# A transformer block on one core: three copies of residuals on GpSimd taken out, with x, x1 and x2 in two buffers each

## The reference, cut to what matters

```
x = x + xattn(ctx, layernorm(x), mask, ...)     # 16 heads of 16, 256 keys from ctx, bias by distance
x = x + attn(layernorm(x), ...)                 # normalizes once more, 16 heads of 64, unit-length q and k,
                                                # two null keys, linear bias, causal
x = x + ffn(layernorm(x), ...)                  # 8 experts of rank 16 on one shared hidden layer of 1024, top 2
return x                                        # (64, 64, 256), float32
```

## Time and profile before

| | |
|---|---|
| Median of 3 runs | 1583.59 us |
| The profiled execution, its own time | 1582.87 us |
| Its span, first to last instruction | 1581.1 us |
| TensorE busy | 1406.5 us, 89% |
| VectorE busy | 1243.2 us, 79% |
| ScalarE busy | 1123.3 us, 71% |
| GpSimd busy | 491.3 us, 31% |
| Mean granted clock of TensorE | 0.968 of full |
| DMA engines, mean rate | 70 GB/s |

### The profile page before, as it was taken

How to read it: one execution, slowest core, us unless ns; L and a number is a source line. 1 busy time by engine, 2 the same in 40 slices (tenths; PEclk the granted TensorE clock), 3 DMA queues, 4 the chain that set the end, 5 groups by cost and what they waited for, 6 DMA issues and landing times.

```text
span 1581.1 us, 42702 instructions
## 1 busy us (share of the span) xinstructions
PE 1406.5 (89%) x16891; PEld 1024.8 (65%) x16891; DVE 1243.2 (79%) x3414; ACT 1123.3 (71%) x3091; POOL 491.3 (31%) x589
## 2 busy tenths in 40 slices
PE   3378999999999999999999999999999999999975
PEld 1245776766677666666776766667666666776744
DVE  2647888888888888888888888888888888888862
ACT  2656778777777787777778777777787777778741
POOL 2122233333323332333233333323332333233220
PEclk7589999999999999999999999999999999999987
DMA  8522212222221122222212222221122222212100
GB/s 199 171 68 75 64 42 63 70 78 79 79 79 47 43 69 78 79 78 79 70 39 60 69 78 79 78 79 53 42 65 78 78 78 79 75 37 57 52 4 7
DMA packets 80918, 110.49 MB, mean 70 GB/s; under 512 B 7592, under 2 KB 62928, under 8 KB 80720
## 3 DMA queue, kind: packets, MB, share of 16 engines
q1 hardware_dynamic: 80720, 107.76, 23.8%
HBM read 69.66 MB, written 29.69 MB: 63 GB/s over the span
## 4 chain that ended last, share of the span: by engine, by line
PE 58%; ACT 29%; DVE 8%; issue 3%; DMA 1%; POOL 1%; SPq 0%; POOLq 0%; ACTq 0%; DVEq 0%
ACT S L924 7%; PE ps_a L507 7%; PE ps_a L508 6%; PE ps_a L509 6%; ACT av L986 5%; ACT pT L936 4%; PE ps_f L507 4%; PE ps_f L509 4%; PE ps_f L508 4%; PE ps_t L597 3%; PE ps_a L728 3%; PE ps_o L609 3%; ACT aqT L1040 3%; ACT a_work L997 2%; PE ps_s L507 2%
## 5 line engine op out<-in xcount | busy, mean ns | idle before, releaser
L924 ACT ACTIVATE S<-S,x_nmx 128x256 f32<-128x256 f32 x512 | 257.0, 506 | 29.9 <-DVE x_nmx L1204 28.3
L1204 DVE CUSTOM_DVE_ANT_0 S<-ps_s,bias 128x256 f32<-128x256 f32 x512 | 201.8, 418 | 65.2 <-PE ps_s L587 63.7
L597 PE MATMUL ps_t<-ident,S 128*128 128x128 f32 x1024 | 188.9, 287 | 42.8 <-ACT S L924 26.3
L1568 POOL TENSOR_TENSOR a_len<-a_len,half 128x16 f32<-128x16 f32 x64 | 212.4, 3318 | 5.3
L936 ACT ACTIVATE pT<-ps_t 128x256 f32<-128x256 f32 x512 | 174.2, 380 | 40.6 <-PE ps_t L597 35.8
L597 PEld LDWEIGHTS ps_t<-ident,S 128*128 128x128 f32 x1024 | 115.3, 143 | 86.3 <-ACT S L924 69.5
L1573 POOL TENSOR_TENSOR aN<-aS,a_sum 128x128 f32<-128x128 f32 x32 | 30.0, 936 | 368.7 <-DVE a_sum L1305 368.7
L587 PE MATMUL ps_s<-kst,qst 128*128 128x256 f16 x512 | 115.5, 279 | 17.8 <-DMA qst<-q_hbm 15.4
L507 PE MATMUL ps_f<-zT,f_loraB 128*128 128x128 f16 x512 | 102.8, 220 | 8.7 <-ACT f_h L1028 8.6
L508 PE MATMUL ps_f<-zT,f_loraB 128*128 128x128 f16 x512 | 102.4, 219 | 0.0
L509 PE MATMUL ps_f<-zT,f_loraB 128*128 128x128 f16 x512 | 102.4, 219 | 0.0
(11 more groups left out here) (244 smaller groups left out, 4643.6 us busy)
## 6 DMA issues: line engine op xcount, KB each, us to landing
ctxT<-in_ctxT SPq DMA_DIRECT2D x32, 512.0 KB, 4.8
k_hbm<-kT SPq DMA_DIRECT2D x32, 512.0 KB, 3.0
kst<-k_hbm SPq DMA_DIRECT2D x32, 512.0 KB, 4.4
kst<-negm SPq DMA_DIRECT2D x32, 256.0 KB, 3.1
q_hbm<-qT SPq DMA_DIRECT2D x64, 128.0 KB, 1.8
kst<-k_hbm SPq DMA_DIRECT2D x32, 256.0 KB, 3.4
qst<-q_hbm SPq DMA_DIRECT2D x32, 256.0 KB, 4.6
x_ld<-in_x SPq DMA_DIRECT2D x32, 128.0 KB, 4.2
```

The lines of the kernel that those rows point to most:

```text
L597: last = turn(ps_t[t % 2][:, c * P:(c + 1) * P], S[:, t % S_BUFS, c * P:(c + 1) * P], ident[:])
L924: go(S[:, t % S_BUFS, :], S[:, t % S_BUFS, :], ACT.Exp, bias=x_nmx[:, t:t + 1], scale=-1.0, accum_out=x_sum[:, t:t + 1]).then_inc(sem["exp ...
L1204: nc.vector.tensor_tensor_reduce(out=S[:, t % S_BUFS, :], in0=ps_s[t % 2][:, 0:TK], in1=bias[:, pair, :], scale=-1.0, scalar=BIG, op0=ALU. ...
L1568: tt(ln, ln, half[:, 0:AH], ALU.pow).then_inc(sem["a_len"], 1)
```

## The change

The three copies on GpSimd, their tiles and their semaphores are gone. `x_ld`, `x1` and `x2` have two buffers each, and unit u uses the one of u % 2. The additions read them directly. The load of x for unit u waits only for x1 of unit u - 2. The tables are new as well: the order of the operations is another one in many places, on all engines. One line of `SLOT` before and now, as a sample; in it `pe_f_first` goes from (15, 39) to (-1, 34), `act_x_split_ctx` from 47 to 9, and `dve_f_norm` from -12 to -14:

```
-    dve_x_merge=(99,), dve_a_residual=(-18,), dve_a_stats=(-28, -19), dve_a_norm=(-22, -11),
...
+    dve_x_merge=(99,), dve_a_residual=(-17,), dve_a_stats=(-28, -19), dve_a_norm=(-21, -16),
```

The code:

```
-        x_ld, x_res, x_n = sb("x_ld", [P, D]), sb("x_res", [P, D]), sb("x_n", [P, D])
+        x_ld, x_n = [sb(f"x_ld{n}", [P, D]) for n in range(2)], sb("x_n", [P, D])
-        x1 = sb("x1", [P, D])
+        x1 = [sb(f"x1_{n}", [P, D]) for n in range(2)]
-        x2 = sb("x2", [P, D])
+        x2 = [sb(f"x2_{n}", [P, D]) for n in range(2)]
...
-                if seen(u - 1):
-                    sp.wait_ge(sem["x_normed"], lone(sp, "x_normed", u - 1, 1))
-                if seen(u - 1):
-                    sp.wait_ge(sem["x_kept"], lone(sp, "x_kept", u - 1, 1))
-                sp.dma_start(x_ld[:], io["x"][bass.ts(u, P), :]).then_inc(sem["x_loaded"], 16)
+                if seen(u - 2):
+                    sp.wait_ge(sem["x1_ready"], at("x1_ready", u - 2, 1))
+                sp.dma_start(x_ld[u % 2][:], io["x"][bass.ts(u, P), :]).then_inc(sem["x_loaded"], 16)
...
             def x_residual(u):
                 dve.wait_ge(sem["xo_done"], at("xo_done", u, 1))
-                dve.wait_ge(sem["x_kept"], at("x_kept", u, 1))
-                if seen(u - 1):
-                    dve.wait_ge(sem["a_kept"], at("a_kept", u - 1, 1))
-                stt(x1[:], ps_o[:, 0:D], DOWN, x_res[:], ALU.mult, ALU.add).then_inc(sem["x1_ready"], 1)
+                stt(x1[u % 2][:], ps_o[:, 0:D], DOWN, x_ld[u % 2][:], ALU.mult, ALU.add).then_inc(sem["x1_ready"], 1)
...
             def a_residual(u):
                 dve.wait_ge(sem["ao_done"], at("ao_done", u, 1))
-                dve.wait_ge(sem["a_kept"], at("a_kept", u, 1))
-                stt(x2[:], ps_a[1][:, 0:D], DOWN, a_res[:], ALU.mult, ALU.add).then_inc(sem["x2_ready"], 1)
+                stt(x2[u % 2][:], ps_a[1][:, 0:D], DOWN, x1[u % 2][:], ALU.mult, ALU.add).then_inc(sem["x2_ready"], 1)
...
-                dve.wait_ge(sem["f_kept"], at("f_kept", u, 1))
-                stt(f_out[:], f_out[:], g_1[:, 3:4], f_res[:], ALU.mult, ALU.add)\
+                stt(f_out[:], f_out[:], g_1[:, 3:4], x2[u % 2][:], ALU.mult, ALU.add)\
...
-            def x_keep(u):
-                pool.wait_ge(sem["x_loaded"], lone(pool, "x_loaded", u, 16))
-                if seen(u - 1):
-                    pool.wait_ge(sem["x1_ready"], lone(pool, "x1_ready", u - 1, 1))
-                pool.tensor_copy(x_res[:], x_ld[:]).then_inc(sem["x_kept"], 1)
```

More of the change, by code:

```diff
@@ new lines @@
+    act_x_spread_q=(-22,), act_x_copy_v=(-11, -9), act_x_split_ctx=(9,), act_x_copy_inv=(89,),
+    act_x_copy_weights=(90,), act_x_exp=(-4, -4, -4, -1, 5, 6, 19, 22, 35, 39, 47, 50, 66, 66, 72, 72),
+    act_x_copy_probs=(-1, 5, 6, 9, 19, 22, 33, 44, 47, 47, 55, 66, 89, 90, 90, 90), act_x_merge=(91,),
+    act_f_copy_turned=(-19,), act_f_exp=(-14,), act_f_copy_z=(-10,), act_f_relu=(-2, 45),
+    act_f_split_hid=(47, 61), act_a_copy_turned=(-22, -16), act_a_copy_k=(-16, -11), act_a_copy_q=(-11, -11),
@@ new lines @@
+    act_x_split_ctx=(96,), act_x_copy_inv=(82,), act_x_copy_weights=(91,),
+    act_x_exp=(-23, -21, -4, 5, 5, 22, 39, 56, 56, 56, 56, 63, 77, 80, 80, 82),
+    act_x_copy_probs=(-1, 21, 23, 23, 45, 47, 47, 62, 65, 65, 82, 83, 83, 83, 83, 86), act_x_merge=(95,),
+    dve_x_split_turned=(-18,), dve_x_split_k=(-26, -23), dve_x_spread_q=(-14,), dve_x_stats=(74,),
+    dve_x_norm=(77,), dve_x_inv=(66,), dve_x_split_inv=(73,),
+    dve_x_bias=(-14, -8, -6, -4, -4, -4, 3, 5, 5, 14, 18, 22, 24, 24, 55, 63), dve_x_merge=(75,),
@@ L245, in build @@
         oT = split("oT", [P, KD, BU, TQ])
-        x1 = sb("x1", [P, D])
-        a_res, a_x, a_n = sb("a_res", [P, D]), sb("a_x", [P, D]), sb("a_n", [P, D])
+        x1 = [sb(f"x1_{n}", [P, D]) for n in range(2)]
+        a_x, a_n = sb("a_x", [P, D]), sb("a_n", [P, D])
         a_st, a_mv, a_rs = sb("a_st", [P, 2, 6]), sb("a_mv", [P, 2, 2]), sb("a_rs", [P, 2, 2])
@@ L264, in build @@
         aP, aN = sb("aP", [P, AH, TQ]), sb("aN", [P, 4, AH, NNULL])
-        x2 = sb("x2", [P, D])
-        f_res, f_n, f_out = (sb(n, [P, D]) for n in ("f_res", "f_n", "f_out"))
+        x2 = [sb(f"x2_{n}", [P, D]) for n in range(2)]
+        f_n, f_out = (sb(n, [P, D]) for n in ("f_n", "f_out"))
         f_st, f_mv, f_rs = sb("f_st", [P, 6]), sb("f_mv", [P, 2]), sb("f_rs", [P, 2])
@@ L1167, in x_stats @@
                 dve.wait_ge(sem["x_loaded"], at("x_loaded", u, 16))
-                stats(u, x_ld[:], x_st[:], x_mv[:], "x_stats", 0)
+                stats(u, x_ld[u % 2][:], x_st[:], x_mv[:], "x_stats", 0)
             def x_norm(u):
                 dve.wait_ge(sem["x_rstd"], at("x_rstd", u, 2))
-                norm(x_ld[:], x_n[:], x_mv, x_rs).then_inc(sem["x_normed"], 1)
+                norm(x_ld[u % 2][:], x_n[:], x_mv, x_rs).then_inc(sem["x_normed"], 1)
             def rest(to, of, less):
@@ L1250, in a_norm @@
             def a_norm(u, k):
-                src, dst = ((x1, a_x), (a_x, a_n))[k]
+                src, dst = ((x1[u % 2], a_x), (a_x, a_n))[k]
                 dve.wait_ge(sem["a_rstd"], at("a_rstd", u, 2 * k + 2))
@@ L1601, in step @@
                             a_length(ua, n)
-                    if do_x:
-                        for n in due(table, "pool_x_keep", s):
-                            if not (isinstance(i, int) and i == 0):
-                                x_keep(i)
-                    if do_a:
-                        for n in due(table, "pool_a_keep", s):
-                            a_keep(ua)
                         for n in due(table, "pool_a_scale_nulls", s):
                             a_scale_nulls(ua)
-                    if do_f:
-                        for n in due(table, "pool_f_keep", s):
-                            f_keep(uf)
                     if ahead:
```

105 lines of the change are left out of this document (43 added, 62 removed).

## The result

The changed kernel takes 1605.22 us in the median of 4 runs (1602.87 to 1606.18), the kernel before 1583.14 on the same chip (4 runs, 1581.47 to 1585.09). The ratio is 1.0141, 95% interval 1.0129 to 1.0154: slower by 22 us. The forecast was 1590, slower by 6.4 than the 1583.59 known then. The profiled execution took 1602.87 us, 20.0 more than the one of before.

A forecast was written before the change was run, and what follows sets the result against it. TensorE bounds each step's first part, then a ScalarE and VectorE chain to the last product. Per step +0.20 + 0.10 = +0.30, times 31 is +9.3; 1582.9 + 9.3 - 1.4 - 0.4 = 1590.4, said 1590; range 1563 to 1606.

The forecast's parts named there:

- The copies at nothing: Three GpSimd copies per unit removed, together 1.24 of 45.5 us; none on the path, so cost 0.
- The rival that they count: Each removed copy frees VectorE or GpSimd's path from the lock: -38.5 us, 1544 us; chance 0.04.
- f_n behind a_n, +0.20: VectorE, first half: a_n goes first, so TensorE waits for f_n before transposing it: +0.20 us per step.
- The stretch to aqT, +0.35: ScalarE from 837.94 to second aqT: ctxS added, three exponentials in a row overlap; second aqT ends +0.35 us.
- The tail, giving back 0.25: Second aqT to last product with V: the reordered work recovers time, so the second half's +0.35 becomes +0.10 us.
- The ends, -1.8 us in the forecast: First and last units' tables: last weight's split earlier, -1.4 us; second pow of a_len earlier, keys' copies later, -0.4 us.
- The won hole: f_first(0) fills TensorE's 0.66 us hole ahead of the first transposed tile, ScalarE catches up: 1566.8 us; chance 0.31.
- The new hole at the second product: Tile 7's copy behind second aS exponential stops TensorE 0.9 us each step, staying to the end: 1618 us; chance 0.13.
- The signs I had named: Changed profile: f_n's transposition waits 0.1 to 0.3 us, first-tile wait gone, aS wait 1.7, period 45.85, first x1 93.4.

The follow-up runs named there:

- the run with the copy put back: Changed kernel with the ctxS copy moved back behind the first aS exponential on ScalarE: 1610.09 us, ratio 1.0173 to the kernel before.
- the kernel with two pieces moved behind aqT: Kernel without the three copies, old order, with x_exp5 and x_copy_probs3 moved behind the query copies aqT on ScalarE: 1649.73 us, ratio 1.0438.
- the kernel with all limits moved: Kernel without copies, old order; key lengths, query scaling and turning earlier, exponential 5 and copy 3 behind aqT, tile 5 and bias 9 later: 1611.69 us, ratio 1.0189.

## Why the prediction was wrong in size

**The copies at nothing: right**, ratio 0.9999 when they go alone. The rival that they count (1544 us) is out. A hold-up of VectorE by GpSimd shows again, elsewhere. GpSimd and VectorE at the end of the step, as in the earlier trace rows:

```profile
872.47 2.14 POOL L1531 TENSOR_TENSOR ctxS<-ctxT,ctxS 128x1024 f16<-128x1024 f32 x1
```

```profile
873.95 0.81 DVE L1160 TENSOR_SCALAR x_n<-x_ld,x_mv,x_rs 128x256 f32<-128x256 f32 x1
```

x_n takes 0.81 us where it took 0.67, and ends 0.15 us behind ctxS in both. That is less than the 0.41 which the same operation takes alone, so the rows do not bear out that the whole of x_n waits, as the prediction read the earlier trace rows; a part of it is done by then. x_n has time to spare there, so nothing comes of it.

**f_n behind a_n, +0.20: right place, too small by 0.15.** It measured +0.35 at the first K product, and +0.34 when undone alone. I had let the three operations keep their total length and only exchanged their places. In the new order a_n and aT start 0.44 apart and not 0.32 to 0.34, and f_n ends 0.13 later than I had it. TensorE starts 0.05 behind that, which is less than the 0.09 I took (-0.04), but then the first K product follows the transposition by 0.50 us and not by 0.44 (+0.06). The trace shows where: before, of the three only aT started no sooner than the operation ahead had ended (828.87 behind 828.84); now a_n and aT both do (838.18 behind 838.14, 838.62 behind 838.59). What makes them wait was not tried.

**The stretch to aqT, +0.35: right in kind, too small by 0.11.** It measured +0.46. The added copy is 0.94 and the wait of 0.25 absorbs its part. All that gives back something in this stretch, the three exponentials in a row among it, is 0.23 to 0.24 and not 0.3; how much of that is theirs was not told apart. The turned queries would have been late as well, as the run with the copy put back shows: with 0.94 less in the stretch aqT came only 0.10 earlier, so some 0.36 of the 0.46 would have stood without the copy. The prediction had them ready at about 27.24 us of the step, near their old 27.12; they came at 27.84, 0.35 of it f_n's.

**The tail, giving back 0.25: wrong by 0.18, and this is the step that failed in its mechanism.** The prediction carried +0.55 at aqT to +0.30 at the last product, on the ground that ctxS no longer stands behind aS, that a tile is done ahead of f_y and that bias 13 comes earlier. Measured, +0.81 at aqT is +0.74 at the last product: 0.07 back. From aqT's end to the last product it is 17.10 us before and 17.03 in the change. With the old tail and the copy out of it (the two experiments in the old order with ctxS forward) it is 16.99, so the new tail gives nothing that the old one would not. The run with the copy put back splits the 0.07: with the copy in it the new tail takes 17.31, 0.21 more than the old one, and taking the copy out gives 0.28. So it was right that ctxS no longer behind aS gives something back; the other moves of the tail, booked as gains beside it, cost. The tile ahead of f_y was not free: it waits 0.18 us for its exponential, and f_y comes 1.03 us later in its step, +0.28 beyond what VectorE's run hands on. That is made good behind it, and no more than that. Which of the other moves costs was not tried one by one.

The right sum of the same terms is 0.35 + 0.46 - 0.07 = 0.74, as the period grew. The forecast had 0.30. Of the 0.44 missing 0.15 is f_n's, 0.11 the stretch's and 0.18 the tail's; in 29 middle steps that is 12.8 us, and the profiled execution took 12.5 more than the 1590.4 of the sum. The ends, -1.8 us in the forecast, gave nothing in the run that had them alone.

The 1605.22 lies in the range of 1563 to 1606, by 0.8 us, but outside the 1581 to 1600 that the forecast took for itself. The range reached beyond 1600 only by the part of a rival that it took in, and no rival's mechanism came about, so that it holds is luck.

**The rivals.** The won hole (1566.8, my 0.31) fell by the run with f_first(0) alone: 1.0007. TensorE's waits behind ScalarE just move. The new hole at the second product is real, 0.54 for the 0.9 expected, but does not stay to the end at its full size: the last product is 0.74 late, as VectorE's run is 0.75. Its price of 1618 did not come, though the result lies closer to it (13 us) than to my own 1590 (15 us). The signs I had named came out so: the transposition of f_n waits for f_n, the hole is gone, aS waits 1.58 for 1.7; the period is 46.28 for 45.85; the first residual comes at 94.3 for 93.4.

## What to carry to other kernels

Undo the order and the code apart before arguing about either: two runs told here that a change named after its copies was wholly one of order. In a pipeline balanced this closely a delay ahead of the longest dependent run goes through nearly whole to the end of each step (0.81 gave 0.74, 0.60 gave 0.49, f_n's 0.34 gave 0.34), so count what is put ahead of the run in full, and book no recovery behind it unless the recovering engine is the one that ends the step. A hole on the busiest engine is worth filling only if the event behind it waits for that engine; ask first which two or three limits lie within a few tenths of a microsecond of it.

## What was not expected of the hardware

The clock, in the kernel with two pieces moved behind aqT. Its windows (columns as in the earlier trace rows) over two neighbouring steps with the same waits, and then over parts of the second:

```profile
234.54:281.48 46.94, 42.95 (x530) 31.51 (x528) 37.83 (x106) 34.49 (x96) 13.98 (x15) 1.00 0.24 66
281.48:331.21 49.73, 45.84 (x530) 33.84 (x528) 37.75 (x106) 34.60 (x96) 13.97 (x15) 0.93 0.22 63
305.48:307.48 2.00, 0.86 (x24) 0.67 (x27) 0.36 (x2) 2.00 (x8) 0.00 (x0) 1.00 0.00 0
307.48:309.48 2.00, 1.47 (x54) 1.17 (x49) 1.94 (x7) 1.30 (x6) 0.00 (x0) 0.71 0.00 0
309.48:311.48 2.00, 2.00 (x37) 1.27 (x31) 1.99 (x6) 1.25 (x3) 0.00 (x0) 0.50 0.00 0
311.48:313.48 2.00, 2.00 (x19) 1.58 (x16) 1.90 (x5) 1.59 (x5) 0.00 (x0) 0.50 0.04 8
313.48:315.48 2.00, 2.00 (x25) 2.00 (x22) 0.67 (x1) 0.00 (x0) 0.00 (x0) 0.58 0.00 0
315.48:317.48 2.00, 1.88 (x36) 1.51 (x34) 0.58 (x1) 1.13 (x2) 0.00 (x0) 1.00 0.00 0
```

Right behind the 1.44 us wait (TensorE busy 0.86 of 2 us) the granted clock falls from 2.4 to 1.2 GHz (1.00 to 0.50 in the rows) and is back some 7 us later. The same wait stands in the step before, where nothing falls. Of the 29 middle steps 14 last 46.93 to 46.95 us and 15 are longer, by 0.3 to 2.8, together 21 us of the 24 that the wait itself does not explain. The clock is 0.93 to 0.97 in the long ones, but for one of 47.22, and 1.00 in the others. Why it falls in some steps and not in others with the same waits is open. In the kernel with all limits moved, where TensorE waits 1.13 us in one place of each step, the clock is 1.00 in all middle steps, and they last 46.38 to 46.83. A wait of TensorE can so cost twice, and a small further step in an order can turn into a large loss.

GpSimd's inverse root of the same 128 x 16 values takes 2.93 us in about half of its instructions (33 of 64 before), 3.72 in nearly all others, and 3.99 in the earlier trace rows. What tells them apart is whether VectorE is already in the scaling of the queries and keys when the root starts. The kernel without the copies in the old order, and then the one with all limits moved:

```profile
838.33 1.22 DVE L1266 TENSOR_TENSOR a_raw<-a_raw,a_len 128x1024 f32<-128x1024 f32 x1 [0.66 <-POOL a_len L1549]
838.62 3.72 POOL L1549 TENSOR_TENSOR a_len<-a_len,half 128x16 f32<-128x16 f32 x1
```

```profile
853.30 2.93 POOL L1553 TENSOR_TENSOR a_len<-a_len,half 128x16 f32<-128x16 f32 x1
854.47 1.22 DVE L1268 TENSOR_TENSOR a_raw<-a_raw,a_len 128x1024 f32<-128x1024 f32 x1
```

In the kernel before, all 31 roots that start during a scaling take 3.72 us or more, and the 33 others 2.93. In all the kernels here these longer roots end 4.0 us after the start of the scaling, whether they start 0.30 us behind it (3.72), 0.15 (3.86) or 0.02 (3.99, as in the earlier trace rows). So the root is held up by the scaling and not slower in itself. The other way round nothing is lost: a scaling that starts during a root takes its usual 1.22. One of the two roots of a step is 0.79 us longer by the order alone, and the kernel with all limits moved is free of that.
